# Three tiles of three, three and two sequences in place of four tiles of two, in a patch-embedding, mLSTM and routed-expert block on one core

## The chip, the core and the metric

The kernel runs on one core of a Trainium2 chip. The metric is the device time of one execution in microseconds (us), taken as the median of several runs. TensorE multiplies matrices, VectorE and ScalarE work on rows and empty the matmul banks, GpSimd does the small powers and issues the DMAs that scatter rows, SyncE issues the plain DMAs.

## The reference, cut to what matters

```python
# 64 images -> 64 sequences of S = 38 tokens (36 patches and two class rows), D = 256
h = patch_embedding(data)                         # B=64, N=36, F=768
h = h + mlstm(layernorm(h))                       # INNER=512, NH=4 heads of 128
#   x_mlstm, z = split(x @ W_up); x_act = swish(causal_conv4(x_mlstm) + b)
#   q, k from x_act, v from x_mlstm (block-diagonal weights), gates i, f per head
#   logD = cumulated log_f differences + i, masked to t <= s within a sequence
#   C = q k^T / sqrt(128) * exp(logD - max);  h = C / max(|sum C|, exp(-max)) @ v
#   per-head norm, skip, swish(z), W_down
h = h + shared_swiglu(ln) + routed_swiglu(ln * sigmoid(top logit))   # top 1 of 32 experts
```

Attention couples the tokens of one sequence only. Rows of two or more sequences can therefore lie in one tile, and a mask takes away what crosses between them.

## The kernel before, in words

**Groups.** The 64 sequences are worked in G = 8 groups of 8, which is GT = 304 token rows. Some stages keep channels on the partitions and all 304 tokens in the free dimension; they know no tiles (embedding, `up`, the convolution, `q_of`, `down`, `gate_up`, `shared_down`). The others keep token rows on the partitions. They cut the group into NT = 4 tiles of TS = 2 sequences, R = 76 rows: the layer norms, `scores`, `v_of`, the gates, `decay` with the exponentials, `weigh`, `heads`, the head norms, routing, ranks, and the scatters to the experts' zones. Turning between the layouts is TensorE's too: `to_rows` (of `h_t`, `att_t` and `ffn_t`), `to_columns` (of `xn` and `xn2`) and `heads_t`.

**Pipeline.** `step(e, f, a, m)` is written once for each engine, and each engine runs its calls in that order. One step embeds group e, does norm, up projection and convolution of group f = e-1, the attention of group a = e-2, and routing and shared experts of group m = e-3. The orders in time come from these hand-written lists and from semaphores. After the eight steps stand two tail steps with orders of their own (a = 6, a = 7), a stretch for the last group's routing, and then the expert phase: 32 experts' slots of 128 rows and five further slots here, one turn each, with weights streamed from memory.

**What the change touches.** `scores(a, j)` makes four products of a 76-row tile into one bank; ScalarE copies them as `c_t`; VectorE sums the gate columns; f_sums, gates_t, the scan `top_gates` and tops_t make the stabiliser; `decay(a, j)` spreads it over a bank; ScalarE takes 16 exponentials (one for each tile and head) into `cw`; `weigh(a, j)` multiplies them with `c_t`; `heads(a, j)` multiplies with `v`. Then VectorE does `norm_2` for pairs of tiles, and `head_stats`, `head_var` tile by tile, GpSimd `rstd_h`, ScalarE `head_norm` of tiles 0 and 1 and VectorE that of tiles 2 and 3, with `last_channel`. TensorE's `heads_t` waits for all of it. In the two tail steps ScalarE does `head_norm` of tile 2 as well.

**Banks and waits.** `f_sums`, `gates_t` and `top_gates` use bank `ab[0]`, which the values of tile 0 have left, and `tops_t` uses `ab[3]`, which tile 3's values have left.

Of the kernel before, what the change touches and what calls it, by code (L numbers as in the profile page):

```python
# [11 lines left out]
S = N + 2  # L12
F = C * P * P
D = 256
# [10 lines left out]
TS = 2  # L25
R = TS * S
NT = GS // TS
TILES = B // TS
HALF = TILES // 2
# [13 lines left out]
Group = namedtuple("Group", "n p")  # L43


def groups_phase(nc, block, patches, w_lin, pos, cols, w_up, conv, chan, wq, wk, wv, wvt, w_gates, b_gates,
# [6 lines left out]
    with ExitStack() as ctx:  # L53
# [236 lines left out]
        CONSTS = 13 + TS + 1  # L290
# [24 lines left out]
        def by_act(n):  # L315

            return NT * NH // 2 * n + NH * max(0, n - (G - 2))

        def by_dve(n):

            return NT // 2 * n - max(0, n - (G - 2))

        @block.sync
        def _(sp):
# [20 lines left out]
            def xs_out(m):  # L345
                sp.wait_ge(s_xs, NT * m.n + NT)
                dst = dram.xs[m.n * GT:(m.n + 1) * GT, :].rearrange("(j p) d -> p j d", p=R)
                sp.dma_start(dst, xs_rows[:]).then_inc(s_xs_out, 16)

            def base_out(m):  # L350
                sp.wait_ge(s_base, 2 * m.n + 2)
                dst = dram.base[m.n * GT:(m.n + 1) * GT, :].rearrange("(j p) d -> p j d", p=R)
                sp.dma_start(dst, base_rows[:, :, 0:D]).then_inc(s_base_out, 16)
# [28 lines left out]
        def _(pool):  # L382
# [16 lines left out]
            pool.affine_select(out=tri[:, S:R], in_=tri[:, S:R], compare_op=ALU.is_ge, fill=0.0,  # L399
                               base=-S, pattern=[[0, S]], channel_multiplier=1).then_inc(s_const, 1)  # L400
# [3 lines left out]
            pool.wait_ge(s_const, 11)  # L404
            pool.tensor_scalar(mask_bf[:], tri[:], -1.0, -MASKED, ALU.add, ALU.mult).then_inc(s_const, 1)
            pool.tensor_copy(ident_bf[:], ident[0:R, 0:R]).then_inc(s_const, 1)
            for s in range(1, TS):
                pool.memset(resets[:, s * S:s * S + 1], MASKED).then_inc(s_const, 1)
            pool.memset(a_gate[:], 0.0).then_inc(s_const, 1)
# [8 lines left out]
            def rstd1_of(f):  # L418
# [3 lines left out]
                pool.tensor_tensor(rstd1[:], rstd1[:], minus_half[:], ALU.pow).then_inc(s_rstd1, 1)  # L422

            def rstd2_of(m):
# [3 lines left out]
                pool.tensor_tensor(rstd2[:], rstd2[:], minus_half[:], ALU.pow).then_inc(s_rstd2, 1)  # L428

            def rstd_h_of(a, j):  # L430

                pool.wait_ge(s_varh, NT * a.n + j + 1)
                pool.tensor_tensor(rstd_h[:, j, :], var_h[:, j, :], minus_half[:],  # L433
                                   ALU.pow).then_inc(s_rstdh, 1)

            def xs_put(m):
# [3 lines left out]
                for j in range(NT):  # L440
                    pool.wait_ge(s_xs, NT * m.n + j + 1)
                    sort.scatter(pool, dram.x_zone, xs_rows[:, j, :], NT * m.n + j, sort.s_x_put)

            def number(m):
                wait(pool, s_base_out, 16 * m.n)
# [4 lines left out]
            def step(e, f, a, m):  # L450
# [3 lines left out]
                if a:  # L454
# [3 lines left out]
                    rstd_h_of(a, 3)  # L458
# [13 lines left out]
        def _(act):  # L472
# [24 lines left out]
            def h_rows_of(f):  # L497
                for b in range(2):
                    act.wait_ge(s_h_mm, 2 * f.n + b + 1)
                    copy(h_rows[:, f.p, 2 * b:2 * b + 2, :].rearrange("p j d -> p (j d)"),  # L500
                         fb[b][0:R, :]).then_inc(s_hrows, 1)
# [22 lines left out]
            def mixed_gates(f, bank):  # L524
                act.wait_ge(s_gm_mm, f.n + 1)
                wait(act, s_gm, 2 * f.n - 1)
                copy(g_parts[:], bank[0:R, GT:GT + 4 * NH * NT]).then_inc(s_gp, 1)
# [8 lines left out]
            def q_of(a):  # L536
                for h in range(NH):
                    act.wait_ge(s_q_mm, NH * a.n + h + 1)
                    act.activation(q_t[:, h, :, 0:R], ab[h][:, 0:GT].rearrange("p (j t) -> p j t", j=NT), ACT.Copy,
                                   scale=float(INNER // NH) ** -0.5).then_inc(s_q, 1)  # L540

            def c_t_of(a, j):
                act.wait_ge(s_c_mm, NT * a.n + j + 1)
                copy(c_t[:, j].rearrange("p h t -> p (h t)"), ab[j][0:R, 0:NH * QW]).then_inc(s_ct, 1)
# [10 lines left out]
            def v_of(a, j):  # L555
                act.wait_ge(s_v_mm, NT * a.n + j + 1)
                copy(v[:, j, :].rearrange("p (h d) -> p h d", h=NH)[:, :, 0:LAST],
                     ab[j][0:R, :].rearrange("p (h d) -> p h d", h=NH)[:, :, 0:LAST]).then_inc(s_v, 1)
# [7 lines left out]
            def decay(a, j):  # L566

                act.wait_ge(s_b_mm, NT * a.n + j + 1)
                for h in range(NH):
                    g = NH * j + h  # L570
                    act.activation(cw[:, j, h, :], ab[j][0:R, h * R:(h + 1) * R], ACT.Exp,  # L571
                                   bias=a_gate[:, g:g + 1]).then_inc(s_dmat, 1)
# [5 lines left out]
            def head_norm(a, j):  # L578
                act.wait_ge(s_rstdh, NT * a.n + j + 1)
                for h in range(NH):  # L580
                    act.activation(o[:, j, h, 0:LAST], ab[j][0:R, h * 128:h * 128 + LAST], ACT.Copy,
# [35 lines left out]
            def step(e, f, a, m):  # L617
# [15 lines left out]
                if a: v_of(a, 3)  # L633
# [1713 lines left out]
```

## Time and profile before

| what | value |
|---|---|
| median of 3 runs | 687.18 us (686.2 to 687.49) |
| the profiled execution | 689.14 us, its span 687.4 us |
| mean granted clock of TensorE | 0.977 of full speed |
| TensorE busy | 634.0 us (92%) in 4029 matmuls, weight loads 535.2 us |
| VectorE busy | 467.2 us (68%) in 1528 instructions |
| ScalarE busy | 391.5 us (57%) in 863 |
| GpSimd busy | 230.0 us (33%) in 249 |

A matmul of 32-bit floats stands in the trace as two instructions. Busy times of TensorE overlap, since matmuls are pipelined: what one costs is read from the start of one to the start of the next. In the lists a row gives start, length, engine, line, operation, names and shapes (for a matmul stationary rows*columns, then the moving operand), how many were merged, and in brackets the idle time ahead with what ended it.

### The profile page before, as it was taken

What the parts mean: (1) busy time and instruction counts of PE and PEld (TensorE: products, weight loads), DVE (VectorE), ACT (ScalarE), POOL (GpSimd) and SP (SyncE); (2) the same over time, 40 slices, a digit from 0 to 9 for tenths busy, and PEclk for the clock granted to TensorE, in tenths of its full rate; (3) what the DMA queues carried; (4) which work ended last, traced back from release to release, by engine and by line L of the source; (5) the groups of instructions that cost most, each with busy time, mean ns of one, the idle gap of its engine ahead of it and who ended that gap; (6) DMA issues with size and microseconds to landing.
All of it is one profiled execution on the core that took longest, in us unless ns stands there. A gap on an engine that the chain in (4) does not pass through costs nothing.

```text
span 687.4 us, 11733 instructions
## 1 busy us (share of the span) xinstructions
PE 634.0 (92%) x4029; PEld 535.2 (78%) x4029; DVE 467.2 (68%) x1528; ACT 391.5 (57%) x863; POOL 230.0 (33%) x249
## 2 busy tenths in 40 slices
PE   5899899999999999999999999888899999999994
PEld 3688778868968967977977988756688888888883
DVE  1644795876776786786686885858577767667761
ACT  0428558529628627636745938514466666666661
POOL 4000210144044054054044241554336666421551
PEclk9999899999999999999999989999999999999998
DMA  8239210030030030022011010155699999999960
GB/s 289 113 92 366 89 53 1 18 92 20 6 103 20 1 99 28 2 54 70 4 32 35 10 33 12 40 181 182 238 410 376 377 381 383 355 303 406 397 225 22
DMA packets 46258, 101.65 MB, mean 148 GB/s; under 512 B 10951, under 2 KB 32245, under 8 KB 41328
## 3 DMA queue, kind: packets, MB, share of 16 engines
q1 hardware_dynamic: 35184, 89.07, 35.9%
q0 software_dynamic: 9488, 8.52, 4.6%
q10 hardware_dynamic: 1520, 3.23, 1.5%
q8 instruction: 35, 0.57, 0.3%
q14 instruction: 31, 0.25, 0.1%
HBM read 80.17 MB, written 23.32 MB: 151 GB/s over the span
## 4 chain that ended last, share of the span: by engine, by line
PE 63%; DVE 16%; ACT 11%; issue 4%; POOL 3%; DMA 3%; SPq 0%; POOLq 0%; DVEq 0%
PE bank L2227 16%; PE bank L1354 10%; PE bank L2246 9%; PE bank L1476 4%; PE bank L1322 4%; DVE stats_h L950 3%; PE bank L1455 3%; PE bank L1418 2%; PE bank L2235 2%; PE bank L1380 2%; PE bank L1331 2%; POOL rstd_h L433 2%; ACT cw L571 2%; ACT hst L552 2%; DVE mv_h L953 2%
## 5 line engine op out<-in xcount | busy, mean ns | idle before, releaser
L433 POOL TENSOR_TENSOR rstd_h<-var_h,minus_half 76x4 f32<-76x4 f32 x32 | 32.3, 1010 | 181.3 <-DVE var_h L964 181.3
L2045 POOL DMA_INDIRECT out<-rows,bg x32 | 37.9, 1185 | 68.0 <-DVE rows L2117 61.1
L2227 PE MATMUL bank<-w_hi,x_hi 128*128 128x512 f32 x148 | 56.5, 463 | 2.9 <-DVE x_lo L2129 2.9
L1322 PE MATMUL bank<-patch,lin_w 128*128 128x288 f32 x192 | 51.3, 420 | 8.3 <-DMA col_t<-cols 7.9
L1322 PEld LDWEIGHTS bank<-patch,lin_w 128*128 128x128 f32 x192 | 36.5, 196 | 19.8 <-issue 10.6
L867 DVE SCALAR_TENSOR_TENSOR y<-xm,conv_t,y 128x296 f32<-128x296 f32 (+2 forms) x96 | 43.7, 510 | 10.1 <-ACT xm L483 10.1
L1816 POOL DMA_INDIRECT x_zone_dram<-xs_rows,spot x32 | 40.2, 1256 | 23.5 <-ACT xs_rows L604 11.4
L1816 POOL DMA_INDIRECT b_zone_dram<-base_rows,spot x32 | 37.7, 1179 | 26.9 <-DVE base_rows L1079 18.4
L2227 PE MATMUL bank<-w_lo,x_hi 128*128 128x512 f32 x148 | 46.3, 394 | 0.0
L2153 DVE TENSOR_TENSOR act_e<-silu_e,bank 128x512 f32<-128x512 f32 x37 | 25.5, 688 | 30.5 <-PE bank L2227 30.5
L2227 PE MATMUL bank<-w_hi,x_lo 128*128 128x512 f32 x148 | 46.1, 393 | 0.0
L2123 DVE TENSOR_TENSOR w_lo<-wts,w_hi 128x1024 fp32r<-128x1024 f32 x36 | 43.1, 1218 | 0.5 <-ACT w_hi L2175 0.5
L2202 ACT ACTIVATE silu_e<-bank 128x512 f32<-128x512 f32 x37 | 22.1, 599 | 34.4 <-PE bank L2227 34.4
L483 ACT ACTIVATE att_t<-bank 128x304 f32<-128x304 f32 x15 | 6.2, 422 | 61.4 <-PE bank L1476 60.9
L1354 PE MATMUL bank<-xn_hi,up_hi 128*128 128x304 f32 x128 | 35.1, 357 | 6.2 <-DVE xn_lo L853 5.9
L2038 POOL DMA_INDIRECT listed_dram<-token,late_spot x32 | 36.4, 1137 | 9.8 <-issue 9.8
L2117 DVE SCALAR_TENSOR_TENSOR rows<-bank,bg 128x256 f32<-128x256 f32 x37 | 15.7, 425 | 31.5 <-PE bank L2246 30.6
L2175 ACT ACTIVATE w_hi<-wts 128x1024 fp32r<-128x1024 f32 x36 | 36.9, 1050 | 0.0
L2170 ACT ACTIVATE x_hi<-bank 128x256 fp32r<-128x256 f32 x37 | 14.2, 384 | 39.7 <-PE bank L2216 39.7
L1536 PE MATMUL bank<-act_t,sd_w 128*128 128x304 f32 x128 | 36.2, 435 | 0.6 <-DVE act_t L1072 0.6
L1455 PE MATMUL bank<-v,cw 76*76 76x128 f32 x256 | 33.3, 287 | 3.0 <-DVE cw L918 2.6
L1354 PE MATMUL bank<-xn_hi,sgu_hi 128*128 128x304 f32 x128 | 31.8, 330 | 3.3 <-DVE act_t L1072 2.8
(254 smaller groups left out, 1776.8 us busy)
## 6 DMA issues: line engine op xcount, KB each, us to landing
wts<-w_exp SPq DMA_DIRECT2D x18, 1024.0 KB, 12.3
x_act<-w_exp SPq DMA_DIRECT2D x10, 1024.0 KB, 11.0
silu_z<-w_exp SPq DMA_DIRECT2D x9, 1024.0 KB, 11.4
wts_down<-w_exp SPq DMA_DIRECT2D x18, 512.0 KB, 10.2
patch<-patches SPq DMA_DIRECT2D x8, 864.0 KB, 6.5
down_w<-w_exp SPq DMA_DIRECT2D x10, 512.0 KB, 10.2
lin_w<-w_exp SPq DMA_DIRECT2D x9, 512.0 KB, 10.8
b_zone_dram<-act_t SPq DMA_DIRECT2D x1, 4160.0 KB, 28.2
```

What stands on the lines that cost most here:

```text
L433: pool.tensor_tensor(rstd_h[:, j, :], var_h[:, j, :], minus_half[:], ALU.pow).then_inc(s_rstdh, 1)
L867: dve.scalar_tensor_tensor(y[:, k, :, lag:], xm[:, f.p, k, :, 0:S - lag], w, y[:, k, :, lag:], ALU.mult, ALU.add).then_inc(s_conv, 1)
L1322: last = pe.matmul(fb[c][:, 0:GS * N], lin_w[:, k, c * 128:(c + 1) * 128], patch[:, k, :], start=(k == 0), stop=(k == KF - 1))
L1354: last = pe.matmul(dst, weights[w][:, c, at:at + 128], x[part][:, c, :], start=(n == 0), stop=(n == 3 * KD - 1))
L1455: last = pe.matmul(ab[j][0:R, h * 128:(h + 1) * 128], cw[:, j, h, :], v[:, j, h * 128:(h + 1) * 128], start=True, stop=True)
L1816: pool.indirect_dma_start(zone, bass.IndirectOffsetOnAxis(ap=self.spot[:, t:t + 1], axis=0), rows, None, bounds_check=E * SLOT - 1, oob_is ...
L2038: pool.indirect_dma_start(dram.listed, bass.IndirectOffsetOnAxis(ap=sort.late_spot[:, t:t + 1], axis=0), sort.token[:, t:t + 1], None, bou ...
L2045: pool.indirect_dma_start(out, bass.IndirectOffsetOnAxis(ap=rows_at, axis=0), rows[:, k % 4, :], None, bounds_check=T - 1, oob_is_err=Fals ...
L2123: dve.tensor_tensor(w_lo[:, k % 2, u, :], wts[k % 4][:, u * KD * I:(u + 1) * KD * I], w_hi[:, k % 2, u, :].bitcast(f32), ALU.subtract).the ...
L2175: act.activation(w_hi[:, k % 2, u, :], wts[k % 4][:, u * KD * I:(u + 1) * KD * I], ACT.Copy).then_inc(s_w_hi, 1)
L2227: last = pe.matmul(banks[2 + 2 * e + u][:, :], x[:, e, c * SLOT:(c + 1) * SLOT], w[:, e, u, c * I:(c + 1) * I], start=(n == 0), stop=(n == ...
L2246: last = pe.matmul(banks[6 + k % 2][:, 0:D], act_et[:, k % 2, c, :], wts_down[k % 4][:, c * D:(c + 1) * D], start=(c == 0), stop=(c == KI ...
```

## The change

Tiles of three sequences: TS = 3, R = 114, NT = 3. The last tile of a group has two sequences (`SHORT` = 76 rows), and every row slice follows `height(j)`. Tiles of all groups are now 24 instead of 32. Calls for tile 3 are gone from all lists. `PAIRS` is tiles 0 and 1, and tile 2 alone. In the two tail steps `head_norm` of tile 2 goes from ScalarE to VectorE.

```diff
-TS = 2
+TS = 3
 R = TS * S
-NT = GS // TS
-TILES = B // TS
+NT = -(-GS // TS)
+TILES = G * NT
+SHORT = GT - (NT - 1) * R
+def height(j):
+    return SHORT if j == NT - 1 else R
+def columns(j):
+    return slice(j * R, j * R + height(j))
+PAIRS = [(slice(0, 2), R), (slice(2, NT), SHORT)]
...
             def by_act(n):
-            return NT * NH // 2 * n + NH * max(0, n - (G - 2))
+            return (NT - 1) * NH * n
             def by_dve(n):
-            return NT // 2 * n - max(0, n - (G - 2))
+            return n
...
             def q_of(a):
                 for h in range(NH):
                     act.wait_ge(s_q_mm, NH * a.n + h + 1)
-                    act.activation(q_t[:, h, :, 0:R], ab[h][:, 0:GT].rearrange("p (j t) -> p j t", j=NT), ACT.Copy,
+                    full = (NT - 1) * R
+                    act.activation(q_t[:, h, 0:NT - 1, 2 * NH:], ab[h][:, 0:full].rearrange("p (j t) -> p j t", t=R),
+                                   ACT.Copy, scale=float(INNER // NH) ** -0.5)
+                    act.activation(q_t[:, h, NT - 1, 2 * NH:2 * NH + SHORT], ab[h][:, full:GT], ACT.Copy,
                                    scale=float(INNER // NH) ** -0.5).then_inc(s_q, 1)
...
             def f_sums(a):
                 pe.wait_ge(s_logf, a.n + 1)
-                pe.wait_ge(s_v, NT * a.n + 1)
-                pe.matmul(ab[0][0:R, 0:NT * NH], tri[:], logf[:].rearrange("p j h -> p (j h)"),
+                pe.matmul(ab[3][0:R, 0:NT * NH], tri[:], logf[:].rearrange("p j h -> p (j h)"),
...
             def decay(a, j):
-                if j == NT - 1:
-                    pe.wait_ge(s_md, a.n + 1)
+                n = height(j)
                 pe.wait_ge(s_v, NT * a.n + j + 1)
-                pe.matmul(ab[j][0:R, 0:GT], ident_bf[:], mask_bf[:].unsqueeze(1).broadcast_to([R, NH, R]),
-                          start=True, stop=False)
+                pe.matmul(ab[j][0:n, 0:NH * n], ident_bf[0:n, 0:n],
+                          mask_bf[0:n, 0:n].unsqueeze(1).broadcast_to([n, NH, n]), start=True, stop=False)
...
             def xs_out(m):
                 sp.wait_ge(s_xs, NT * m.n + NT)
+                for b, (tiles, rows) in enumerate(PAIRS):
+                    ...  # one DMA for the first two tiles, one for the last; base_out alike
...
             (step of TensorE; the other lists alike)
                     heads(a, 2)
-                    heads(a, 3)
...
-            pe.wait_ge(s_const, CONSTS)        # now ahead of the first h_rows_of
             pe.wait_ge(s_w_emb, 3 * 16)
```

Also changed: `mixed_gates` and `route` read their results out of the bank in two instructions, one for each height; GpSimd clears, at the start, the rows of some tiles that nothing writes; and in the expert phase `list_late` runs over 24 tiles.

## Rows read from the trace of the kernel before

**Rows 1.** Busy time by stretch (us): four steady steps, tail, expert phase, and the tail's slow stretches.

```profile
155.00:208.70 53.70, 50.97 (x374) 43.72 (x373) 39.48 (x163) 32.09 (x84) 15.83 (x18) 1.00 0.14 41
481.40:660.00 178.60, 176.65 (x869) 145.69 (x870) 125.09 (x170) 111.68 (x167) 87.27 (x78) 1.00 0.98 363
...
397.70:404.20 6.50, 6.47 (x35) 6.50 (x36) 4.79 (x14) 1.47 (x4) 0.00 (x0) 0.53 0.01 3
```

**Rows 2.** Chain of waits through one steady step, 208.69 to 262.54: start, us.

```profile
208.69 2.32 PE bank L1418 x32
...
226.32 0.48 DVE cw L918
...
229.66 1.75 PE bank L1455 x16
...
239.27 0.47 DVE act_t L1072
...
249.42 1.24 PE bank L1465 x16
...
261.66 0.87 PE bank L1331 x8
```

**Rows 3.** TensorE in time, same step: short products, and the turning of the heads.

```profile
214.34 1.04 PE L1391 MATMUL bank<-v_w,xm 128*76 128x128 f32 x8
...
221.47 0.29 PE L1496 MATMUL bank<-route_w,xn_lo 128*76 128x32 f32 x2
221.61 0.30 PE L1493 MATMUL bank<-route_w,xn_hi 128*76 128x64 f32 x2
...
249.42 1.24 PE L1465 MATMUL bank<-ident,o 76*128 76x76 f32 x16 [1.14 <-DVE o L969]
```

**Rows 4.** Chain of waits, 44 to 156: 16 products with 128 stationary and 8 moving columns.

```profile
47.59 1.83 PE bank L1307 x16
```

**Rows 5.** ScalarE in time, same steady step.

```profile
225.33 3.50 ACT L571 ACTIVATE cw<-bank,a_gate 76x76 f32<-76x76 f32 x16
...
243.68 0.43 ACT L522 ACTIVATE silu_z<-bank 128x304 f32<-128x304 f32 x1
```

**Rows 6.** VectorE in time, same step: the fourth tile's work.

```profile
245.51 0.16 DVE L964 TENSOR_TENSOR var_h<-var_h,square_h 76x4 f32<-76x4 f32 x1
...
245.66 0.87 DVE L950 BATCH_NORM_STATS2 stats_h<-bank 76x6 f32<-76x127 f32 x4
...
247.40 0.68 DVE L974 TENSOR_TENSOR o<-bank,rstd_h 76x508 f32<-76x508 f32 x1
...
249.12 0.15 DVE L969 SCALAR_TENSOR_TENSOR o<-mv_h,rstd_h 76x4 f32<-76x4 f32 x1
```

**Rows 7.** VectorE and GpSimd groups by shape: count | busy, mean ns | idle before.

```profile
L1072 DVE TENSOR_TENSOR act_t<-silu_g,bank 128x304 f32<-128x304 f32 x32 | 15.0, 468 | 11.4 <-ACT silu_g L610 7.4 <-PE bank L1354 3.8
L918 DVE TENSOR_TENSOR cw<-c_t,cw 76x304 f32<-76x304 f32 x32 | 14.9, 470 | 18.2 <-ACT cw L571 18.2
...
L997 DVE TENSOR_TENSOR h<-bank,h_rows 76x512 f32<-76x512 f32 x16 | 10.3, 681 | 18.4 <-PE bank L1331 18.4
...
L1860 DVE TENSOR_TENSOR o<-hot,start_row 76x1024 f32<-76x1024 bf16 x1 | 1.2, 1216 | 0.0
```

**Rows 8.** GpSimd groups by shape.

```profile
L1816 POOL DMA_INDIRECT x_zone_dram<-xs_rows,spot x32 | 40.2, 1256 | 23.5 <-ACT xs_rows L604 11.4 <-issue 8.4 <-DVE spot L1058 3.6
L2045 POOL DMA_INDIRECT out<-rows,bg x32 | 37.9, 1185 | 68.0 <-DVE rows L2117 61.1 <-issue 6.0 <-POOL take L2089 1.0
...
L433 POOL TENSOR_TENSOR rstd_h<-var_h,minus_half 76x4 f32<-76x4 f32 x32 | 32.3, 1010 | 181.3 <-DVE var_h L964 181.3
```

**Rows 9.** Chain of waits, 44 to 156: where the second attention begins.

```profile
84.26 0.68 DVE o L974
...
99.30 1.32 DVE stats L1006 x4
...
107.67 1.71 PE bank L1391 x8
```

**Rows 10.** Chain of waits, tail step a = 6: the fourth tile's values ahead of the exponentials.

```profile
379.34 0.48 ACT v L483
379.84 1.28 ACT L571
```

**Rows 11.** TensorE in time in the two tail steps: the waits for the head norms.

```profile
397.73 2.26 PE L1465 MATMUL bank<-ident,o 76*128 76x76 f32 x16 [1.08 <-DVE o L969]
...
444.00 1.61 PE L1465 MATMUL bank<-ident,o 76*128 76x76 f32 x16 [1.39 <-DVE o L969]
```

**Rows 12.** Chain of waits, end of the last group.

```profile
472.71 1.42 POOL x_zone_dram L1816
```

**Rows 13.** TensorE in time: the last group's rows, and the first expert.

```profile
478.67 1.07 PE L1331 MATMUL bank<-ident,ffn_t 128*76 128x128 f32 x8 [0.29 <-ACT ffn_t L483]
480.02 0.44 PE L2216 MATMUL bank<-ident,xg 128*128 128x128 f32 x2 [0.28 <-DMA xg<-x_zone_dram]
```

More of the change, by code:

```diff
@@ L497, in h_rows_of @@
             def h_rows_of(f):
-                for b in range(2):
+                for b, (tiles, rows) in enumerate(PAIRS):
                     act.wait_ge(s_h_mm, 2 * f.n + b + 1)
-                    copy(h_rows[:, f.p, 2 * b:2 * b + 2, :].rearrange("p j d -> p (j d)"),
-                         fb[b][0:R, :]).then_inc(s_hrows, 1)
+                    dst = h_rows[0:rows, f.p, tiles, :].rearrange("p j d -> p (j d)")
+                    copy(dst, fb[b][0:rows, 0:dst.shape[-1]]).then_inc(s_hrows, 1)
             def xn_t_of(f):
@@ L927, in norm_2 @@
             def norm_2(a, b):
-                tiles = slice(2 * b, 2 * b + 2)
+                tiles, rows = PAIRS[b]
                 done = 8 * a.n + 4 * b
@@ L994, in h2_of @@
             def h2_of(a):
-                for b in range(2):
+                for b, (tiles, rows) in enumerate(PAIRS):
                     dve.wait_ge(s_at_mm, 2 * a.n + b + 1)
-                    dve.tensor_tensor(h2[:, a.p, 2 * b:2 * b + 2, :],
-                                      ab[2 + b][0:R, :].rearrange("p (j d) -> p j d", j=2),
-                                      h_rows[:, a.p, 2 * b:2 * b + 2, :], ALU.add).then_inc(s_h2, 1)
+                    made = ab[2 + b][0:rows, 0:(tiles.stop - tiles.start) * D].rearrange("p (j d) -> p j d", d=D)
+                    dve.tensor_tensor(h2[0:rows, a.p, tiles, :], made, h_rows[0:rows, a.p, tiles, :],
+                                      ALU.add).then_inc(s_h2, 1)
             def ln2_stats(m):
@@ L1074, in base_of @@
             def base_of(m):
-                wait(dve, s_base_out, 16 * m.n)
+                wait(dve, s_base_out, 32 * m.n)
                 wait(dve, sort.s_b_put, 16 * NT * m.n)
-                for b in range(2):
+                for b, (tiles, rows) in enumerate(PAIRS):
                     dve.wait_ge(s_ft_mm, 2 * m.n + b + 1)
-                    dve.tensor_tensor(base_rows[:, 2 * b:2 * b + 2, 0:D],
-                                      mb[b][0:R, :].rearrange("p (j d) -> p j d", j=2),
-                                      h2[:, m.p, 2 * b:2 * b + 2, :], ALU.add).then_inc(s_base, 1)
+                    made = mb[b][0:rows, 0:(tiles.stop - tiles.start) * D].rearrange("p (j d) -> p j d", d=D)
+                    dve.tensor_tensor(base_rows[0:rows, tiles, 0:D], made, h2[0:rows, m.p, tiles, :],
+                                      ALU.add).then_inc(s_base, 1)
             def step(e, f, a, m):
@@ L1136, in step @@
                     last_channel(a, 2)
-                    head_norm(a, 3)
-                    last_channel(a, 3)
                 if f and f.n == 1:
@@ L1189, in _ @@
             conv_of(f, 0, (1,))
+            head_norm(a, 2)
             last_channel(a, 2)
-            head_norm(a, 3)
-            last_channel(a, 3)
             rank_of(m)
@@ L1326, in to_rows @@
             def to_rows(dst, src, done):
[L1328 to L1329 removed]
+                for b, (tiles, rows) in enumerate(PAIRS):
+                    for j in range(NT)[tiles]:
                         for c in range(KD):
[L1331 to L1332 removed]
+                            last = pe.transpose(dst[b][0:rows, (j % 2) * D + c * 128:(j % 2) * D + (c + 1) * 128],
+                                                src[:, c, columns(j)], ident[:])
                     last.then_inc(done, 1)
             def h_rows_of(f):
+                if f.n == 0:
+                    pe.wait_ge(s_const, CONSTS)
                 pe.wait_ge(s_ht, KD * f.n + KD)
@@ L1417, in scores @@
                 for h in range(NH):
-                    last = pe.matmul(ab[j][0:R, h * QW:(h + 1) * QW], x_act[:, a.p, h, j * R:(j + 1) * R],
-                                     q_t[:, h, j, :], start=True, stop=True)
+                    last = pe.matmul(ab[j][0:n, h * w:(h + 1) * w], x_act[:, a.p, h, columns(j)],
+                                     q_t[:, h, j, 0:w], start=True, stop=True)
                 last.then_inc(s_c_mm, 1)
```

254 lines of the change are left out of this document (127 added, 127 removed).

## The prediction

> **What bounds the kernel now.** I read the busy times by stretch first. A steady step takes 53.70 us with TensorE busy 50.97 and VectorE 39.48; the expert phase is TensorE from end to end, 176.65 of 178.60 us [rows 1]. No turn of an expert has tiles in it, so that phase only starts earlier. What the change can give is in eight attention steps and the ends around them. TensorE's 95% hides two things: its matmuls overlap, and the short ones are cheap or dear by what they wait for. So I went on with the chain of waits through one steady step, 208.69 to 262.54 [rows 2]. It leaves TensorE four times: for the gates' exponentials (ScalarE) ahead of the values, for the decay's exponentials and `weigh` ahead of `heads`, for VectorE's long run of head statistics ahead of `heads_t`, and for h2 ahead of the next step. The reader is to see that removing an instruction pays only where its engine is then the last one. TensorE in time shows the largest stall: `heads_t` starts 1.14 us late, with VectorE's `o` ending it [rows 3].
>
> **The steady step, part by part.** All numbers are start to start.
>
> Up to the first `up` product, tile 3's values are multiplied and copied, but the chain there is ScalarE's table loads and `xn_hi`, which stay; their removal pays nothing. `scores` takes 2.32 us for 32 instructions [rows 2], 0.0725 each for 84 columns. A product with 128 columns takes 1.75/16 = 0.109 [rows 2], so 122 columns take some 0.104: 16 x 0.104 + 8 x 0.0725 = 2.24. Gain 0.08.
>
> The decay's exponentials: 16 in 3.50, 0.21 each; ScalarE with 304 columns takes 0.43 [rows 5], about 1 ns a column, so 114 columns take 0.245. The first tile is ready 4 x 0.035 = 0.14 later. `weigh` grows from 304 to 456 columns; 304 take 0.47 and 512 take 0.68 [rows 7], so it grows by 0.16. Heads 0 start 0.3 later. Heads 1 wait for their own exponentials, 0.98 after heads 0 and not 0.87: 0.1 more. Then 8 products of heads 3 are gone, 8 x 0.109 = 0.87. Net gain here 0.47. ScalarE ends its exponentials 0.55 earlier, so what follows on it does not hold this back. `ranks` has one product less, 0.05.
>
> Route and mixed gates have 16 products each, which become 12, but they gain nothing. They are bound by their stationary side: 0.0685 each with 76 stationary columns, be it 32 or 64 moving ones (221.47 to 221.61 is two) [rows 3], and 1.83/16 = 0.114 with 128 [rows 4]. Between the two, 114 take 0.102: 8 x 0.102 + 4 x 0.0685 = 1.09 against 1.10. The Trainium skill (TensorE: Matmul & The Clock Gate, LDWEIGHTS) says the same against this change: a weight load costs by its columns, not its rows, columns over 1.2 per ns, an estimate of 95 ns for 114. The trace's 0.102 stands near it. A reader who counts instructions alone would book 4 x 0.0685 twice, 0.55 us a step.
>
> `down`, `up`, the convolution and the turns to columns keep their column counts and their time.
>
> Next comes the stretch of the head norms. Let T0 be the end of `expert_act` 3, at 239.74 [rows 2]. Before, VectorE runs from T0 to 249.27, where the last `last_channel` ends [rows 6]. The change takes away tile 3's statistics and variance (245.66 to 247.4, 1.75), one copy, one `last_channel`. The variance of tile 2 is ready at T0 + 5.9 [rows 6], GpSimd takes 1.01 [rows 8] and 0.1 of waits, `head_norm` and `last_channel` 0.75: T0 + 7.75. TensorE's own work comes to `heads_t` at T0 + 8.55 (249.42 less 1.14), less 0.22 for two of the eight instructions of `ffn_rows` (8 take 0.87 [rows 2]): T0 + 8.3. The embedding in it still waits for `silu_z` 2 at 243.68 [rows 5], behind tile 0's head norm and now behind two copies of the gates instead of one, 0.1 more. So TensorE takes over as the last one, at T0 + 8.3 to 8.4, against T0 + 9.68. Gain 1.3 of the 1.75 removed.
>
> `h_rows_of` again loses 0.22. The second half of h2 falls from 512 to 256 columns: 0.68 [rows 7] for 0.42, gain 0.27. `q_of` has two copies for each head instead of one, 0.1 us more for each; `h_rows_of` on TensorE covers it (0.65), and without that cover it would cost 0.2.
>
> Sum for a steady step: 0.08 + 0.47 + 0.05 + 1.3 + 0.22 + 0.27 = 2.4. Four of them: 9.6.
>
> **The unusual stretches.** Start: `h_rows`, statistics and `xn` of group 0 lose one tile of four, about 0.33 + 0.1 + 0.4: 0.9. That TensorE no longer waits for the constants gives nothing, since it starts with the loads; it also covers GpSimd's added clearing. First attention and start of the second: the chain there is VectorE's to 84.26 and on [rows 9], so the full 1.8 shows; statistics of both norms and `xn` lose a tile each (four take 1.32 [rows 9]), 1.05 together; tile 3's values, 8 instructions in 1.71 in front of `up` [rows 9], are on the path there, 0.9; h2 and h_rows 0.4; less 0.15 for longer exponentials: 4.0. The rest of the second step is as a steady one, 2.3.
>
> Tail step a = 6: ScalarE's table load for the exponentials directly follows the copy of tile 3's values, 0.48 [rows 10], so the exponentials end 0.48 + 0.55 earlier, and VectorE's run behind them is 1.8 shorter. `heads_t` at 397.73 had waited 1.08 [rows 11]. VectorE would allow 2.85 less. TensorE's own stream loses 0.87 of `heads`, and the `silu_z` for which its gates wait moves with ScalarE's 1.05, so it arrives 1.2 earlier; with the wait gone that is 2.3. Then `att_rows` 0.2: 2.5. Step a = 7 likewise: 1.39 of wait [rows 11], 0.87 of `heads`, 0.4 of smaller waits on VectorE, and 0.4 in the rows after it: 3.0. After the wait in a = 6 the granted clock is 0.53 for 6.5 us [rows 1], the lower level of 1.2 GHz for most of it, and `heads_t`'s 16 turns take 2.26 where the steady step takes 1.24 [rows 2, 11]. If the wait goes, I expect the slow stretch to go: 2.2 more. For a = 7 other waits stay; I book nothing.
>
> Last group: norm and `xn` of one tile (0.6), routing's small operations (0.4), h2 and base 0.5, ffn_rows 0.2, and on GpSimd one scatter of four less, 1.42 + 0.30 [rows 12]. TensorE ends its `ffn_rows` 0.28 before the first expert's rows are there [rows 13], so the scatter counts only as far as TensorE also moves: 2.0 in all. Expert phase: `late_rows` handles 768 instead of 1024 columns, twice 1.22 us [rows 7] in turns where TensorE waits for VectorE: 0.5.
>
> Sum: 0.9 + 4.0 + 2.3 + 9.6 + 2.5 + 3.0 + 2.2 + 2.0 + 0.5 = 27.0. The profiled execution goes from 689.14 to 662.1. The median lies 1.96 below that execution: 687.18 - 27.0 = **660.2 us**.
>
> **What the trace doesn't show.** Nothing has 114 rows. For VectorE, 128 rows cost as 76 (468 and 470 ns at 304 columns [rows 7]). A scatter of 128 rows costs 1.19 and of 76 rows 1.26 [rows 8], so 24 replace 32 at the same price. GpSimd's power has only 76 rows; its bounds are 1.01 and, in proportion to rows, 1.5. I take 1.01, as its scatters do not grow; at 1.5 VectorE's T0 + 7.75 becomes 8.25, still under TensorE's. ScalarE lies between 1.0 and 1.5 times; at 1.5 the exponentials take 4.2 for 3.5 and the gain of `heads` is lost, 1.2 a step, 9 us in all. TensorE short products: if 114 stationary columns cost as 128, 16 x 0.012 in route and gates, 1.5 us in all.
>
> **Rivals.**
> (A) *Absorbed*: coarser tiles. Each of the few waits is for a larger piece, and ScalarE becomes the last engine ahead of `heads` or in the banks' hand-over. For it: the chain leaves TensorE four times a step. Against: ScalarE is busy 32 of 53.7 us [rows 1]. At ScalarE's upper bound and without the clock's 2.2: 27 - 9 - 2.2 = 16 us gained, 671.
> (B) *More*: the tail's second slow stretch goes too, about 1.7 us, and the cold 1.71 of [rows 9], 0.8, with 0.3 a step for smaller waits that I did not follow: 32 us gained, 655.
> (C) *Slower*: the clock. TensorE loses 2.2 us of work a step, and if this made it fall in every step as in a = 6, a stretch of that kind costs 1.0 in `heads_t` and 1.8 in the products after it, 2.8; it decides only from 27/8 = 3.4 a step on, 689 and more. Against: all steady steps ran at 1.00 with a wait of 1.14 in each [rows 1, 3], and that wait goes.
> (D) *Nothing*: the fourth tile was off the path everywhere. The 1.14 and 1.75 us above speak against it; it would take the waits going to ScalarE, 685 to 688.
>
> **How the numbers follow.** Forecast 0.55, A 0.22, B 0.16, C 0.04, D 0.03. The range reaches from B, 653, to A, 672. Differences under 0.2% (1.4 us) can't be told from none here. Faster: 0.55 + 0.22 + 0.16 and a part of D, 0.94. Same 0.02, slower 0.04.
>
> **What would show it.** Right: steady steps of about 51.4 us; `heads_t` without a VectorE wait; heads 0 waiting 0.3 longer for `cw`; route's 12 products still 1.1 us; `weigh` at 0.63; `rstd_h` near 1.01; clock 1.00 after a = 6. Wrong: exponentials over 0.3 each, `rstd_h` at 1.5, new waits on `q_t` ahead of `scores`, a clock under 1 in a steady step, or an expert phase longer than the 178.6 us between its marks.

## The result and the profile after

| | before | after |
|---|---|---|
| median of the runs (lowest to highest) | 687.22 us (686.2 to 687.49, 4 runs) | 663.69 us (662.69 to 669.96, 4 runs) |
| profiled execution, and its span | 689.14, 687.4 us | 662.69, 661.0 us |
| ratio of after to before, 95% interval | | 0.968, 0.964 to 0.973 |
| a steady step (start of `scores` to start of `scores`) | 53.85 us | 51.37 us |
| the first expert's start to the end of the span | 206.0 us | 206.5 us |

The change takes 23.5 us off the median. From profiled execution to profiled execution it is 26.45 us, where the prediction summed 27.0. The two figures differ because the profiled execution of before lay 1.92 us above this median (1.96 above the 687.18 of the prediction), and that of after is the quickest of its four, 1.0 below theirs. It is also the one with the highest mean granted clock, 0.990; the three others have 0.975 to 0.981.

The busy time by stretch, two steady steps, the former slow stretches behind the last two turnings of the heads, and the expert phase and its end (columns as in [rows 1]):

```profile
147.80:199.20 51.40, 48.29 (x322) 41.46 (x323) 34.61 (x139) 30.56 (x82) 13.24 (x15) 1.00 0.14 43
199.20:250.60 51.40, 48.30 (x322) 41.46 (x323) 34.62 (x139) 30.59 (x82) 13.27 (x15) 1.00 0.15 43
378.60:385.00 6.40, 6.40 (x44) 5.70 (x43) 5.91 (x18) 2.60 (x8) 1.33 (x2) 1.00 0.08 18
420.00:425.00 5.00, 4.95 (x29) 3.77 (x28) 4.36 (x13) 1.48 (x4) 1.85 (x2) 1.00 0.23 67
454.40:633.00 178.60, 177.14 (x873) 146.26 (x874) 124.43 (x170) 112.30 (x168) 77.93 (x69) 1.00 0.99 363
633.00:661.00 28.00, 18.02 (x89) 14.61 (x87) 10.52 (x15) 8.17 (x13) 7.32 (x7) 0.88 0.18 49
```

Against [rows 1] a steady step has 2.3 us less in it, TensorE 2.7 us less work and VectorE 4.9 us less. The clock is 1.00 behind the turning of the heads in step a = 6, where it had been 0.53. The 0.88 of the last row costs nothing: it comes from a stretch that begins when TensorE has no product left (see the expert phase below). The chain of waits through one steady step, the counterpart of [rows 2]:

```profile
199.12 2.42 PE bank L1447 x24
...
206.96 0.87 DVE xn_lo L878 x2
207.87 1.10 PE bank L1382 x6
...
217.03 0.65 DVE cw L944
217.72 2.12 PE bank L1482 x16
...
229.21 0.47 DVE act_t L1111
229.68 0.81 DVE stats_h L978 x4
...
231.44 1.05 POOL rstd_h L456
...
233.80 0.32 ACT silu_z L544
...
234.25 3.15 PE bank L1347 x12
237.40 0.66 PE bank L1356 x6
```

The reader is to see that after the last `act_t` the chain no longer stays with VectorE through four tiles of statistics. It follows the first tile's through GpSimd and ScalarE to the embedding's `silu_z`, and from there TensorE runs through. TensorE in time shows the same, the counterpart of [rows 3]:

```profile
207.87 0.55 PE L1382 MATMUL bank<-xn_hi,up_hi 128*128 128x304 f32 x2 [1.83 <-DVE xn_lo L878]
...
212.30 0.36 PE L1521 MATMUL bank<-route_w,xn_hi 128*114 128x64 f32 x2
212.50 0.35 PE L1524 MATMUL bank<-route_w,xn_lo 128*114 128x32 f32 x2
212.70 0.30 PE L1521 MATMUL bank<-route_w,xn_hi 128*76 128x64 f32 x2
212.84 0.29 PE L1524 MATMUL bank<-route_w,xn_lo 128*76 128x32 f32 x2
...
217.72 2.12 PE L1482 MATMUL bank<-v,cw 114*114 114x128 f32 x16 [0.37 <-DVE cw L944]
...
237.90 1.21 PE L1493 MATMUL bank<-ident,o 114*128 114x114 f32 x12
```

`heads_t` (L1493) waits for nobody. Two things are new: the first `up` product (L1382) waits 1.83 us for VectorE's `xn_lo`, where the kernel before waited 0.47 us at the same place of a steady step, and `heads` wait 0.37. VectorE in time, for [rows 6] and [rows 7], then the group of GpSimd's power, for [rows 8]:

```profile
217.03 0.63 DVE L944 TENSOR_TENSOR cw<-c_t,cw 114x456 f32<-114x456 f32 x1 [1.71 <-ACT cw L602]
...
233.83 0.88 DVE L978 BATCH_NORM_STATS2 stats_h<-bank 76x6 f32<-76x127 f32 x4
...
236.69 0.68 DVE L1005 TENSOR_TENSOR o<-bank,rstd_h 76x508 f32<-76x508 f32 x1 [0.97 <-POOL rstd_h L456]
237.30 0.15 DVE L999 SCALAR_TENSOR_TENSOR o<-mv_h,rstd_h 76x4 f32<-76x4 f32 x1
```

```profile
L456 POOL TENSOR_TENSOR rstd_h<-var_h,minus_half 114x4 f32<-114x4 f32 (+1 forms) x24 | 24.4, 1015 | 179.0 <-DVE var_h L993 179.0
```

### The profile page after: what moved, and what is told of

It is laid out like the page before. It is cut to its first block, busy times and chain, and to the rows that moved or that the text cites. A ratio compares the mean times of both kernels' runs of the same rounds, so it can differ in the third digit from the quotient of the medians.

```text
span 661.0 us, 10632 instructions
## 1 busy us (share of the span) xinstructions
PE 604.0 (91%) x3613; PEld 507.0 (77%) x3613; DVE 429.6 (65%) x1338; ACT 376.6 (57%) x839; POOL 196.5 (30%) x226
## 4 chain that ended last, share of the span: by engine, by line
PE 69%; ACT 13%; DVE 12%; issue 3%; POOL 1%; DMA 1%; SPq 0%; DVEq 0%; ACTq 0%; POOLq 0%
PE bank L2244 16%; PE bank L1382 11%; PE bank L2263 9%; PE bank L1347 7%; PE bank L1504 4%; PE bank L1447 3%; PE bank L1482 3%; PE bank L1408 2%; PE bank L2252 2%; PE bank L1564 2%; PE bank L1356 2%; ACT hst L581 2%; ACT L594 2%; ACT L592 2%; ACT cw L602 2%
## 5 line engine op out<-in xcount | busy, mean ns | idle before, releaser
L456 POOL TENSOR_TENSOR rstd_h<-var_h,minus_half 114x4 f32<-114x4 f32 (+1 forms) x24 | 24.4, 1015 | 179.0 <-DVE var_h L993 179.0
L1382 PE MATMUL bank<-xn_hi,up_hi 128*128 128x304 f32 x128 | 34.1, 349 | 14.4 <-DVE xn_lo L878 14.3
L1832 POOL DMA_INDIRECT b_zone_dram<-base_rows,spot x24 | 31.1, 1296 | 26.9 <-DVE base_rows L1119 20.9
L1832 POOL DMA_INDIRECT x_zone_dram<-xs_rows,spot x24 | 30.2, 1260 | 20.5 <-DVE spot L1097 8.5
L1382 PEld LDWEIGHTS bank<-xn_hi,up_hi 128*128 128x128 f32 x128 | 20.5, 198 | 18.0 <-DVE xn_lo L878 13.0
L1382 PE MATMUL bank<-xn_hi,sgu_hi 128*128 128x304 f32 x128 | 31.0, 323 | 3.5 <-DVE act_t L1111 3.0
L1504 PE MATMUL bank<-hst,down_w 128*128 128x304 f32 x128 | 34.1, 420 | 0.1
```

Of the source, the lines that this page charges most:

```text
L1382: last = pe.matmul(dst, weights[w][:, c, at:at + 128], x[part][:, c, :], start=(n == 0), stop=(n == 3 * KD - 1))
L1504: last = pe.matmul(ab[c][:, 0:GT], down_w[:, k, c * 128:(c + 1) * 128], hst[:, k, :], start=(k == 0), stop=(k == KI - 1))
L1832: pool.indirect_dma_start(zone, bass.IndirectOffsetOnAxis(ap=self.spot[0:n, t:t + 1], axis=0), rows[0:n, j, :], None, bounds_check=E * SLO ...
```

## The experiments

Each kernel was run beside the kernel before on the same chip; the time given is the median. The marks are the starts of `scores` and of `heads_t` in TensorE's trace.

**1. VectorE's fourth tile put back.** The function is called ahead of `norm_2(a, 1)` in every attention step. Nobody reads what it writes.

```
+            def fourth(a):
+                dve.wait_ge(s_pv_mm, NT * a.n + NT)
+                for h in range(NH):
+                    dve.bn_stats(more_s[0:SHORT, h, :], ab[2][0:SHORT, h * 128:h * 128 + LAST]).then_inc(s_more, 1)
...
+                    dve.bn_aggr(more_m[0:SHORT, h, :], more_s[0:SHORT, h, :]).then_inc(s_more, 1)
...
```

> The changed kernel, and on VectorE in every attention step, ahead of the short tile's statistics, the statistics and variance of one more tile, written where nobody reads them (4 statistics, 4 aggregations, 3 small operations: about 1.68 us by the first tile's in the trace after, 229.60 to 231.28). Theory (VectorE's run would be last again ahead of the turning of the heads): it ends about T0 + 9.4 in a steady step while TensorE arrives at T0 + 8.36, so the turning waits about 1.1 us in each of the eight attention steps, 8.8 us in all, and if the two slow stretches of the clock come back with the waits of the last two groups, 3.6 us more: 672 to 676 us. Rival (the gain came from TensorE's own stream, VectorE is not near the path): 663 to 665 us, and no wait on VectorE ahead of the turning.

Measured: 681.62 us. TensorE's waits summed by place (us in all, times, longest), then one of them in time:

```profile
PE bank L1505 <- DVE cw L948: 4.3, 5, 2.6
PE bank L1516 <- DVE o L1019: 8.8, 7, 1.8
```

```profile
193.05 1.24 PE L1516 MATMUL bank<-ident,o 114*128 114x114 f32 x12 [1.18 <-DVE o L1019]
```

The wait of `heads_t` is back, 8.8 us in 7 waits, where the changed kernel has 0.2 in one and the kernel before 8.2 in 7. The undisturbed steady step (152.85 to 205.59) lasts 52.74 us, 1.36 more. The expectation set TensorE's arrival at T0 + 8.36; by the rows it is 237.90 less 229.68, T0 + 8.22, so 1.2 was due and 1.18 came. At a = 7 the turning waits for nothing (the waits are those of a = 0 to 6); the added work shows there in a longer wait for `act_t`. The total went beyond the expected 672 to 676. Three of the steady steps also had the clock at 0.50 for 3.4 us, 1.0 to 1.7 us each, and the first profile of the changed kernel has neither the slow stretch of 6.8 us at 71.7 nor the one of 3.4 us ahead of a = 7's turning that stand here. The stretches in steady steps are taken up in experiment 9.

**2. The same at a = 6 alone.** (`if not (a.n == G - 2): return` ahead of it.)

> The same extra work on VectorE, in the attention of the last group but one alone (a = 6). The turning of the heads there started at 378.57 without a wait, VectorE's last operation for it ended at 378.03, so it should now wait about 1.1 us. Theory that the wait brings the slow clock: the stretch behind it shows a granted clock of about 0.5 again, and the turning of the next group starts 3 to 3.5 us later than 420.13. Rival (the clock fell for another reason, and the wait alone counts): clock 1.00 behind it and 1.0 to 1.2 us. Second rival (the tail absorbs it): under 0.3 us. Total 664 to 667 us.

Measured: 667.02 us. `heads_t` at a = 6 waits 1.11 us for VectorE, and the clock behind it stays up:

```profile
384.00:390.50 6.50, 6.50 (x42) 5.77 (x43) 5.75 (x17) 2.04 (x5) 1.43 (x2) 1.00 0.08 20
```

The step lasts 42.42 us and not 41.15. The wait brings no slow stretch behind it. It costs more than itself, though: in the next step TensorE waits 2.22 us for VectorE's `act_t` and not 1.50, and the turning of a = 7 comes 2.0 us later in all, where the first rival had 1.0 to 1.2. No run explains that part. On the clock the first rival holds, and the prediction's reason for its 2.2 us does not.

**3. The same at a = 3 alone.**

> The same extra work on VectorE, in one steady step alone (a = 3, the step from 199.0 to 250.4 in the trace after). Theory: the turning of the heads waits about 1.1 us in that step, the step lasts 52.5 us in place of 51.4, the clock stays at 1.00, every later mark is 1.1 us later. Rival (TensorE's stream is what counts): 51.4 us, no wait. If the wait brings a slow stretch in a steady step as well, 54 to 55 us and a clock under 1.00 behind it.

Measured: 667.05 us. The turning waits 1.18 us, from `heads_t` to `heads_t` it is 52.73 us in place of 51.37, and the clock is 1.00 behind it. As expected, with 0.2 us of further delay ahead of the wait, as in experiment 1, whose cause is open. (The step behind it has a slow stretch of 3.4 us, see experiment 9.)

**4. The second tile's products of weights and values made twice.**

```
-                for h in range(NH):
+                for h in range(NH) if j != 1 else tuple(range(NH)) * 2:
```

> The changed kernel with the second tile's four products of weights and values made twice (the same values again): as many such products in a step as before the change, 16. Theory (TensorE's stream sets the step): 4 products of 4 passes over 128 columns at the spacing of the trace, about 0.85 us a step, 0.9 less the 0.37 us that the first tile's products wait if these come early, in eight steps 6 to 7 us: 669 to 671 us. Rival (they lie in a wait): under 1.5 us, 664 to 665 us.

Measured: 673.82 us (670.56 to 678.34), the profiled execution 670.56. By stretch:

```profile
202.30:254.60 52.30, 49.20 (x332) 42.33 (x330) 34.79 (x139) 30.63 (x82) 13.32 (x15) 1.00 0.14 42
254.60:307.60 53.00, 50.28 (x331) 43.73 (x330) 34.89 (x139) 30.53 (x82) 13.22 (x15) 0.97 0.14 42
```

A step with the clock at 1.00 is 52.22 us from mark to mark, 0.85 more. The four products of the second tile pay in full, even in a kernel whose `heads` wait 0.37 us ahead of them.

**5. The part for VectorE alone, on the kernel before.** Its fourth tile's four statistics and four aggregations are left out, so that tile is normed with zeros as mean and variance; all else is as before.

```
                 dve.wait_ge(s_pv_mm, NT * a.n + j + 1)
+                if j == 3:
+                    return
                 for h in range(NH):
                     dve.bn_stats(stats_h[:, j, h, :], ab[j][0:R, h * 128:h * 128 + LAST]).then_inc(s_sth, 1)
```

> The kernel before, with VectorE's four statistics and four aggregations of the fourth tile left out (its mean and variance are then zeros; all else is done), 1.26 us less by those rows. This is the part of the change that concerns VectorE alone. Theory (VectorE's run was last ahead of the turning of the heads): the turning waited 1.14 us in a steady step, VectorE's run now ends about 1.3 us earlier, so the wait is gone and each of the eight attention steps is 1.0 to 1.2 us shorter, 8 to 9.5 us in all, plus up to 3.6 us if the slow stretches behind the last two groups' waits go with them: 674 to 679 us. Rival (TensorE's own stream gives the gain): 686 to 687 us.

Measured: 681.74 us, ratio to the kernel before 0.993 (0.990 to 0.995). The total misses the expected 674 to 679, and so does the step: it is 53.10 us, 0.75 shorter and not 1.0 to 1.2. VectorE in time, then TensorE:

```profile
246.50 0.68 DVE L977 TENSOR_TENSOR o<-bank,rstd_h 76x508 f32<-76x508 f32 x1 [0.64 <-POOL rstd_h L434]
247.10 0.15 DVE L972 SCALAR_TENSOR_TENSOR o<-mv_h,rstd_h 76x4 f32<-76x4 f32 x1
247.47 0.68 DVE L977 TENSOR_TENSOR o<-bank,rstd_h 76x508 f32<-76x508 f32 x1 [0.22 <-POOL rstd_h L434]
```

```profile
248.37 1.24 PE L1468 MATMUL bank<-ident,o 76*128 76x76 f32 x16 [0.39 <-DVE o L972]
```

With four tiles GpSimd's powers, one a tile and 1.01 us each [rows 8], stand in a row, and once VectorE's statistics are gone VectorE waits for them, 0.64 and 0.22 us where the kernel before waited 0.37 once. So of 1.26 us only 0.75 came out. The change removes a power too; that it thereby gets past this is argued. At a = 6 of this profile TensorE waits 0.24 us ahead of the turning, and a slow stretch of 3.4 us lies behind it all the same (0.74 from 394.3 to 400.8).

**6. The second tile's values made twice** (the edit of 4, in `v_of`).

> The changed kernel with the second tile's four value products made twice (the same values again), as many as before the change. The prediction booked the removal of four such products in a step at nothing, since TensorE waits for ScalarE's chain (two table loads) right behind them: 1.83 us at 207.87. Theory: the 0.85 us lie in that wait, the wait is 1.0 us, a steady step stays at 51.4 us, total 663 to 666 us. Rival (they are on the path): 0.85 us a step, some 6.5 us in all, 670 us.

Measured: 666.63 us. From `scores` to the first `up` it is 8.83 us in both kernels (250.41 to 259.24, and 253.90 to 262.73), a steady step 51.36. In a steady step the four products cost nothing, as booked. At a = 7 they cost 0.81 us: from `scores` to `heads_t` it is 26.65 us, and 25.84 in both profiles of the changed kernel, all at a clock of 1.00. So values were worth something there, where the prediction booked none. The expectation was wrong on where they lie in a steady step:

```profile
262.73 0.55 PE L1382 MATMUL bank<-xn_hi,up_hi 128*128 128x304 f32 x2 [1.74 <-DVE xn_lo L878]
```

That wait shrank by 0.09 us alone; of the rest the trace shows 0.27, the wait for `xn` ahead of it, which is gone.

**7. The changed kernel and the kernel before, again.**

> The changed kernel unchanged, as a yardstick for the runs beside it on the same chip: 663 to 666 us. In the trace the question is where the clock is granted at 0.50. If such stretches belong to the added waits of the earlier experiments, there is none in the steady steps here; if they belong to the chip, they stand here too, each some 0.8 to 1.7 us, and the total is nearer 666 us.

> The kernel before, unchanged, for a second profile. Is the slow stretch behind the turning of the heads of the last group but one (396.9, 6.8 us at 0.50) there again, and the one of the last group (444.7)? If they belong to the kernel, both are there; if to that execution, they are gone or elsewhere, and the gain that the prediction booked for them is no part of the change. Steady steps 53.8 to 53.9 us in either case where the clock is 1.00. 686 to 689 us. One look.

Measured: 665.93 us (662.96 to 666.44, 5 runs) for the changed kernel, ratio 0.967 (0.965 to 0.969); 688.9 us for the one execution of the kernel before. The changed kernel by stretch, two steps with a slow stretch in them and one without; then the kernel before, a steady step and the stretch behind `heads_t` of a = 6:

```profile
149.40:200.80 51.40, 48.68 (x317) 42.33 (x316) 34.67 (x139) 29.81 (x79) 12.65 (x13) 0.97 0.15 43
201.50:254.20 52.70, 49.51 (x323) 42.93 (x321) 34.60 (x139) 30.58 (x82) 13.26 (x15) 0.97 0.14 42
211.00:214.50 3.50, 3.50 (x17) 3.50 (x16) 1.25 (x6) 1.69 (x4) 0.00 (x0) 0.52 0.02 10
305.60:357.00 51.40, 48.31 (x323) 41.45 (x322) 34.66 (x139) 30.58 (x82) 13.24 (x15) 1.00 0.09 25
```

```profile
208.50:262.50 54.00, 51.09 (x375) 43.92 (x374) 39.51 (x163) 32.20 (x84) 16.01 (x18) 1.00 0.14 41
398.50:405.00 6.50, 6.50 (x46) 5.78 (x47) 5.78 (x17) 2.44 (x6) 1.36 (x2) 1.00 0.04 10
```

Both answers matter. The slow stretch of a = 6 in the kernel before, 0.53 in [rows 1], is not there in a second execution of the same kernel, whose waits ahead of `heads_t` are the same 8.2 us in 7 times: it was that execution's and not the kernel's. Without it the step a = 6 lasts 43.92 us in the kernel before, against 45.50 with it and 41.15 to 41.17 in the changed kernel: the stretch cost 1.6 us, and the change gives 2.8 there by itself. And the changed kernel has slow stretches of its own in steady steps, which its first profile did not show: those steps last 52.17 and 52.67 us, 0.8 and 1.3 more.

**8. Wait and short products together at a = 6.** Experiment 2, with the short tile's turnings and gate products made twice in that step.

> The changed kernel with, in the attention of the last group but one alone, the extra statistics on VectorE of the earlier experiment (a wait of about 1.1 us ahead of the turning of the heads), the short tile's four turnings made twice (16 in all) and the short tile's narrow gate products made twice, as there were before. If the amount of short products together with the wait brings the slow clock behind the turning, it is granted 0.50 there again, as in the kernel before, and the next group's turning starts 3 us or more later than those 2 us of added work account for. If not, the clock is 1.00 there, and what brought it in the kernel before stays open. One look.

Measured: 668.69 us in one execution. The wait is 0.86 us, and the clock from 383.9 to 390.4 is 1.00. What brought the slow stretch in [rows 1] stays open.

**9. The new wait ahead of `up` filled.** In the first profile of the changed kernel no steady step had a slow stretch; in the six other profiles of kernels with this wait at 1.8 us (experiments 1 to 4, 6, and the changed kernel again) and in experiment 8 there were one to three, always from 9.1 to 10.6 us after the step's first `scores`, just behind that wait (14 stretches in all, so more than the expectation below counts). None of the two profiles of the kernel before, nor experiment 5, had one in a steady step.

```
                 if m: to_columns(mb, xn2, s_xn2, m.n, s_xn2t_mm)
+                if f and f.n > 1: stream(ab[3], lin_w, 2)
                 if f: up(f, 0)
```

> The changed kernel with TensorE's wait ahead of the new group's first product (1.82 us in a steady step) filled by two products of 128 x 512 that nobody reads, from the third group on; nothing else waits less or more. In the seven profiles so far of kernels with this wait at 1.8 us, the changed kernel's own second profile among them, six or more stretches of steady steps were granted 0.50 of the clock for 3.4 us right behind it, each making its step 0.8 to 1.3 us longer; the two profiles of the kernel before, whose wait there is 0.47 us, had none. Theory (the longer wait brings them): none in the steady steps here, all of them 51.4 us, and a total of 662 to 665 us with the slower executions gone (the changed kernel's own had a median of 665.9 beside the last experiments). Rival (they come by chance or from the chip): one or two are there again, 664 to 667 us. If the two products are too long for the wait, each step is some 0.1 to 0.3 us longer.

Measured: 670.05 us (668.51 to 670.7), ratio 0.971 (0.969 to 0.973). One steady step and the tail by stretch:

```profile
303.50:354.80 51.30, 49.96 (x326) 42.04 (x325) 34.67 (x139) 30.48 (x82) 13.14 (x15) 1.00 0.09 25
364.50:374.70 10.20, 10.20 (x53) 10.03 (x52) 4.56 (x23) 7.10 (x20) 0.00 (x0) 0.50 0.00 1
```

All four steady steps are 51.36 us and none has a slow stretch, as the theory said. But the total is a miss. A stretch of 10.2 us at the lower of the two levels, 1.2 GHz, now lies in the tail step a = 6, which lasts 46.00 us in place of 41.15, and one of 3.4 us in a = 7, which takes 1.3 us more up to its turning. They cost more than those that went. The fill does not stand in the tail steps, which have orders of their own; but the waits just ahead of the 10.2 us are 0.51 and 0.39 us, the same as in the first profile of the changed kernel, which has no slow stretch there. So this slow stretch has no long wait just ahead of it.

**10. ScalarE's order changed, twice.** ScalarE stands in the chain of waits ahead of the `up` product and ahead of `heads`. Its rows there, in the changed kernel:

```profile
206.03 0.57 ACT L505 ACTIVATE v<-bank 114x508 f32<-114x508 f32 x1
206.51 0.73 ACT L505 ACTIVATE xn_hi<-bank 128x304 fp32r<-128x304 f32 x2
...
211.92 1.86 ACT L581 ACTIVATE hst<-x_act,chan_t 128x304 f32<-128x304 f32 x4
...
215.90 2.90 ACT L602 ACTIVATE cw<-bank,a_gate 114x114 f32<-114x114 f32 x12
```

The first edit moves the copy of the second tile's values (the first of these rows) behind the two copies for `up`.

```
                     v_of(a, 0)
                     log_f(a)
+                if f: xn_t_of(f)
+                if a:
                     v_of(a, 1)
-                if f: xn_t_of(f)
-                if a: v_of(a, 2)
+                    v_of(a, 2)
```

> The changed kernel with ScalarE's copy of the second tile's values moved behind the two copies that TensorE's first product of the new group waits for (1.83 us of waiting at 207.87). Theory (ScalarE's order sets that wait): the product starts about 0.48 us earlier, ScalarE idles 0.67 us behind it anyway, so each of six steps is up to 0.48 us shorter: 2 to 3 us in all, 661 to 662 us where the changed kernel takes 663.7. Rival (the wait moves to the first tile's product of weights and values, which waits 0.37 us for VectorE already): no difference within 0.5 us.

Measured: 661.09 us (659.54 to 664.75), ratio 0.962 (0.959 to 0.965). The steady step is 50.87 us, 0.50 shorter; the wait ahead of `up` is 1.35 us. The theory holds and the rival falls. The second edit keeps the first and moves the four scalings (`hst` above) as well:

```
-                if a: skip_of(a)
                 if f: xm_of(f, 3)
...
                     silu_g_of(m, 0)
-                    silu_g_of(m, 1)
+                if a: skip_of(a)
+                if m: silu_g_of(m, 1)
```

> As v1, and ScalarE's four scalings of the skip path (1.75 us) moved from ahead of the exponentials to behind the first SiLU of the experts' gate, where ScalarE idled 1.71 us. Theory: the weights come 1.7 us earlier, the 0.37 us wait of the product of weights and values goes too, and a step is 0.8 us shorter than the changed kernel's: 5 us in all over six steps, 658 to 660 us. Rival (the second SiLU comes late and TensorE waits for it, or another wait of ScalarE takes the place): same as v1 or worse, 661 to 664 us.

Measured: **657.63 us** (654.12 to 658.89), ratio to the kernel before 0.955 (0.952 to 0.958), against 0.967 (0.965 to 0.969) of the changed kernel beside it on the same chip. ScalarE in time, and a steady step by stretch:

```profile
216.57 0.42 ACT L643 ACTIVATE silu_g<-bank 128x304 f32<-128x304 f32 x1
216.89 1.86 ACT L581 ACTIVATE hst<-x_act,chan_t 128x304 f32<-128x304 f32 x4
219.45 0.42 ACT L643 ACTIVATE silu_g<-bank 128x304 f32<-128x304 f32 x1 [0.70 <-PE bank L1383]
```

```profile
197.30:247.40 50.10, 47.87 (x323) 41.35 (x322) 34.67 (x139) 30.67 (x82) 13.24 (x15) 1.00 0.15 44
```

The four scalings fit in ScalarE's idle time, 0.70 us of it is left, `heads` wait no more in a steady step, and the step is 50.10 us, 1.27 less where 0.8 was expected. This version beats both kernels. Neither of the two has a slow stretch in a steady step; both have one in the tail step a = 6, of 10.2 us (the first) and 6.8 us (the second), as in experiment 9.

## Why the prediction was right, and where it was not

By stretch, in us of profiled execution. The measured gains are differences between the same marks of the two traces: `scores` of a = 0 (52.28 before, 50.84 after), of a = 2 (154.68, 147.66), of a = 6 (370.09, 353.14), of a = 7 (415.60, 394.29), the first expert's first product (481.39, 454.44) and the end of the span.

| stretch | forecast | measured |
|---|---|---|
| start | 0.9 | 1.44 |
| first attention and second step | 6.3 | 5.58 |
| four steady steps | 9.6 | 9.93 |
| a = 6, with the clock | 4.7 | 4.36 |
| a = 7 and the last group | 5.0 | 5.64 |
| expert phase | 0.5 | -0.5 |
| sum | 27.0 | 26.46 |

The 5.58 is not all the change's: the kernel before has 10.2 us of slow stretches there in both its profiles, the changed kernel 3.4 in its first and 6.8 in its second. The two second profiles (experiment 7) give 5.26 for it. In a = 7, of these four profiles, only the first of before has one (3.4 us).

Inside a steady step the five pieces between marks came out as worked:

| from, to | before | after | gain | forecast |
|---|---|---|---|---|
| `scores`, first `up` | 8.78 | 8.83 | -0.05 | 0.08 |
| first `up`, `heads` 0 | 9.54 | 9.85 | -0.31 | -0.3 |
| `heads` 0, T0 | 12.90 | 11.96 | 0.94 | 0.87 + 0.05 - 0.1 |
| T0, `heads_t` | 9.68 | 8.22 | 1.46 | 1.3 |
| `heads_t`, next `scores` | 12.95 | 12.51 | 0.44 | 0.49 |

**VectorE was the last engine ahead of `heads_t`: shown**, from both sides (experiments 1, 3 and 5). Its run now ends at 237.45, T0 + 7.77 (forecast 7.75), and TensorE arrives at T0 + 8.22 (8.3 to 8.4). **The removed value products are worth nothing in a steady step: shown** (6); at a = 7 they are worth 0.81, which the prediction left out of its 3.0. **The removed `heads` products pay in full: shown** (4: 0.85 for four).

**The costs of 114 rows**, unmeasured before, came at the lower bound or near it, but for `scores`: `weigh` 0.63 us with 456 columns, GpSimd's power 1015 ns, twelve exponentials 2.90 us, a scatter 1.26 to 1.30. `scores` itself: 24 instructions take 2.35 us, from their first to the product that follows them (199.04 to 201.39), where 2.24 was the sum and 32 had taken 2.32, so its gain of 0.08 was none. Route takes from 211.98 to 212.98 for 12 products, 1.00 us where 1.09 was worked out: two products with 114 stationary columns start 0.20 apart, 0.100 each, be their moving side 64 or 32 columns. By that the trace agrees with the Trainium skill (TensorE: Matmul & The Clock Gate, LDWEIGHTS), whose rule gave an estimate of 95 ns. The products saved brought 0.1 us and not 0.27.

**The step that failed is the clock of a = 6.** The prediction booked 2.2 us because "if the wait goes, I expect the slow stretch to go". The stretch did go, but not for that reason: an added wait of 1.11 us there does not bring it (2), nor with the short products as well (8), and a second execution of the kernel before has the wait and not the stretch (7). The number was right by the choice of executions compared. With the second profile of before, a = 6 gives 2.8 us against 2.5 forecast without the clock, and the stretch was worth 1.6 and not 2.2. What brings a slow stretch stays open. By the same token the slow stretch behind a = 7's turning, which rival B named and the forecast left out, is no sure gain either.

**Rival C was half right.** The steady steps did not fall as it said, behind `heads_t`. But a clock under 1 in a steady step, one of the prediction's own signs of being wrong, did come: the changed kernel's longer wait ahead of `up`, which no part of the prediction listed, is followed in most profiles by a slow stretch or two, about 2.1 us in the second profile (0.8 and 1.3), where the median was 665.93. That the wait brings them is suggested by the counts, and by experiment 9 as far as the steady steps go, but not shown. Why a longer one then appears in a = 6, behind waits of 0.51 and 0.39 us alone, and why the first profile has neither, is not explained.

**The 3.5 us between 660.2 and 663.69** are three things: the forecast carried over the 1.96 us by which before's profiled execution lay above its median, the sum was 0.55 us too large, and after's median lies 1.0 us above its profiled execution.

**The expert phase** was to gain 0.5 and lost 0.5. TensorE's part of it did gain: from the first expert's first product to the end of TensorE's last one it takes 198.13 us before and 197.31 after, 0.8 less. The loss lies behind that last product, in the last rows and their scatter, 7.90 us before and 9.21 after. TensorE's last products, before and after:

```profile
677.55 1.97 PE L2246 MATMUL bank<-down_w,act_et 128*128 128x256 f32 x8 [0.73 <-issue]
```

```profile
649.79 1.97 PE L2263 MATMUL bank<-down_w,act_et 128*128 128x256 f32 x8 [0.73 <-issue]
```

This end varies from execution to execution: the second profile of the kernel before has 8.91 us there, and the kernels with tiles of three sequences 7.53 to 9.21. So the loss can't be laid to the change. Nor is it the clock: every profile has a stretch at half the clock at the very end, of 5.3 to 8.6 us, but it begins only after the last product (683.7 before, 654.5 after), where TensorE has nothing to do.

## What to carry to other kernels

Larger tiles pay by the instruction only on the engine that is last at the next hand-over: here four tiles to three gave TensorE its `heads` products in full, VectorE 1.46 of 1.75 us, and the values nothing in a steady step; cut the step at its hand-overs and ask at each which engine comes last. After such a change read the chain again: the waits had moved to ScalarE's order, and two moved calls brought another 8 us on the same chip, with nothing removed. And before a gain is booked on a clock that one profile shows, take a second profile of the same kernel.

## What the runs showed of the hardware

The same kernel, executed twice, had TensorE's clock at half in different places: the kernel before had 6.8 us of it behind `heads_t` of a = 6 once and none there the other time, with spans of 687.4 and 687.2 us. With TensorE kept busy through a wait of 1.8 us in each step, by products that nobody reads, the steady steps had no slow stretch, and the kernel was no faster: 670.05 us against 665.93 for the unfilled one on another chip, ratios to the kernel before beside them 0.971 (0.969 to 0.973) and 0.967 (0.965 to 0.969). Its profile shows a stretch of 10.2 us at the lower level in a later step, behind waits of 0.51 and 0.39 us.
